# A state-space stage whose side work is moved in its schedule: pieces read two units behind, two silus and the low rank part at other units

## What is computed

```python
xz = x @ Wi.T
xp, z = (xz[..., :d_inner], xz[..., d_inner:])
xp = silu(causal_conv4(xp, conv_w) + conv_b)
dlt, Bp, Cp = split(xp @ Wx.T, [64, 80])         # the low rank part
delta = softplus(dlt @ Wdt.T + bdt)              # the time steps
h[t] = exp(delta[t] * A) * h[t-1] + delta[t] * Bp[t] * xp[t]
y[t] = sum_n Cp[t, n] * h[t, n] + xp[t] * Dp
out = y * silu(z) @ Wo.T
```

## Time and profile before

| | before |
|---|---|
| median of 3 runs | 1148.64 us (1146.84 to 1153.44) |
| profiled execution | 1147.67 us |
| its span | 1145.9 us |
| busy PE / PEld / DVE / ACT / POOL | 873.2 / 561.9 / 883.2 / 631.6 / 735.1 us |
| mean granted clock of TensorE | 0.856 |

### The profile page before, as it was taken

How to read it: one execution, slowest core, us unless ns; L and a number is a source line. 1 busy time by engine, 2 the same in 40 slices (tenths; PEclk the granted TensorE clock), 3 DMA queues, 4 the chain that set the end, 5 groups by cost and what they waited for, 6 DMA issues and landing times. The chain is left out here.

```text
span 1145.9 us, 14984 instructions
## 1 busy us (share of the span) xinstructions
PE 873.2 (76%) x4244; PEld 561.9 (49%) x4244; DVE 883.2 (77%) x1786; ACT 631.6 (55%) x1407; POOL 735.1 (64%) x508
## 2 busy tenths in 40 slices
PE   7897959897989587862899928697979887259920
PEld 4243324333434243432799904365656676259920
DVE  5796999799989999978577755795986977455412
ACT  4878735875587558426344413747385774256610
POOL 0889799889898999920766466665323442047656
PEclk8899989997999898975899958799899977569965
DMA  5644445455445444523233412202001110332223
GB/s 160 186 117 139 150 151 166 128 160 165 138 146 160 151 152 154 170 89 108 61 93 93 80 53 72 64 27 71 21 29 47 47 48 19 105 132 66 68 67 98
DMA packets 90905, 118.95 MB, mean 104 GB/s; under 512 B 12508, under 2 KB 48804, under 8 KB 90696
## 3 DMA queue, kind: packets, MB, share of 16 engines
q1 hardware_dynamic: 84168, 104.34, 29.3%
q0 software_dynamic: 6656, 13.64, 4.9%
HBM read 103.70 MB, written 14.25 MB: 103 GB/s over the span
## 5 line engine op out<-in xcount | busy, mean ns | idle before, releaser
L695 POOL TENSOR_TENSOR ma_bu<-ma_u,ma_row_b 128x1024 f32<-128x1024 f32 x128 | 298.4, 2357 | 9.6 <-DVE ma_u L896 8.0
L415 PE MATMUL y_ps<-ma_h,ident 128*128 128x512 f32 x512 | 259.5, 646 | 26.5 <-POOL ma_h L705 21.5
L570 ACT ACTIVATE decay_ps<-ma_delta,negA 128x512 f32<-128x512 f32 x256 | 172.4, 686 | 83.0 <-DVE ma_h L790 80.1
L1228 POOL DMA_INDIRECT s_rows<-xs,take x112 | 125.3, 1119 | 131.4 <-POOLq L950 83.5
L415 PEld LDWEIGHTS y_ps<-ma_h,ident 128*128 128x128 f32 x512 | 102.3, 208 | 160.1 <-issue 113.4
L1245 PE MATMUL s_up_ps<-s_xt,s_w 128*128 128x128 f32 x896 | 121.3, 280 | 0.0
L780 DVE TENSOR_TENSOR_SCAN decay_ps<-decay_ps,ma_carry,ma_bu 128x512 f32<-128x512 f32 x88 | 110.1, 1271 | 11.2 <-issue 8.4
L1581 POOL TENSOR_TENSOR mi_dec<-mi_dec,mi_gm 128x512 f32<-128x512 f32 x32 | 40.7, 1273 | 120.2 <-DVE mi_gm L2046 107.3
L790 DVE TENSOR_TENSOR ma_h<-decay_ps,ma_row_c 128x512 f32<-128x512 f32 x176 | 117.2, 666 | 0.0
L1245 PEld LDWEIGHTS s_up_ps<-s_xt,s_w 128*128 128x128 f32 x896 | 112.1, 196 | 0.0
L705 POOL TENSOR_TENSOR ma_h<-ma_h,ma_row_c 128x1024 f32<-128x1024 f32 x40 | 97.0, 2425 | 20.6 <-DVE ma_h L780 18.7
(11 more groups left out here) (324 smaller groups left out, 1735.9 us busy)
## 6 DMA issues: line engine op xcount, KB each, us to landing
ma_row_b<-bc_rows SPq DMA_DIRECT2D x128, 256.0 KB, 3.6
ma_row_c<-bc_rows SPq DMA_DIRECT2D x128, 256.0 KB, 3.3
mi_cs<-cs_rows SPq DMA_DIRECT2D x32, 256.0 KB, 3.3
ys<-s_outs SPq DMA_DIRECT2D x28, 256.0 KB
w<-in_experts SPq DMA_DIRECT2D x1, 4112.0 KB, 14.9
w<-in_experts SPq DMA_DIRECT2D x1, 3072.0 KB, 10.9
xs<-rows SPq DMA_DIRECT2D x4, 512.0 KB, 3.4
out<-X SPq DMA_DIRECT2D x8, 256.0 KB, 2.3
```

Of the source, the lines that this page charges most:

```text
L415: mm = pe.matmul(y_ps[:, j, :], m.ident[:], h[g % HS][:, j, :], start=False, stop=True, skip_group_check=True)
L570: act.activation(decay[s % DS][:], delta[b % 2][:, j, col(c)], ACT.Exp, scale=m.negA0[:, j, n:n + 1]).then_inc(decay_done, 1)
L695: pool.tensor_tensor(bu[g % BUS][:], u[b % 2][:, :, col(c)], both(row_b[g % BS]), ALU.mult).then_inc(bu_done, 1)
L1228: pool.indirect_dma_start(rows[s % ROWS][:], None, m.xs[layer], bass.IndirectOffsetOnAxis(ap=m.take[:, s:s + 1], axis=0)).then_inc(fetched ...
```

## The change

Five sets of unit numbers change, and ACT reads the pieces of unit g-2 in its unit g, where it read those of g-1 (across the border of a batch too):

```diff
-    Z, XP = (5, 6, 8, 11), (4, 7, 10, 13)
-    Z_SILU, X_SILU, LOW, V, SOFT, SUM, U = 12, 14, 16, 18, 23, 25, 27
+    Z, XP = (5, 7, 9, 11), (4, 6, 8, 10)
+    X_SILU, Z_SILU, LOW, V, SOFT, SUM, U = 12, 16, 13, 16, 21, 23, 25
+    READ_AFTER = 2
     GATE, OUT, COUNT = (18, 1), (22, 2), (24, 5)
...
-    FIRST_HAT = {2: 9, 3: 17}
-    FIRST_TURN = {2: 14, 3: 24}
+    FIRST_HAT = {2: 9, 3: 23}
+    FIRST_TURN = {2: 20, 3: 27}
...
-                    if s > 0:
-                        for key in pieces(b, s - 1):
+                    if g >= READ_AFTER:
+                        for key in pieces(*divmod(g - READ_AFTER, UNITS)):
                             read_piece(key)
```

## The result

| | before | after |
|---|---|---|
| median of 4 runs each | 1150.35 us (1146.84 to 1153.44) | 1178.1 us (1174.96 to 1182.97) |
| ratio, with 95% interval | | 1.0246 (1.0193 to 1.0299) |
| profiled execution | 1147.67 us | 1174.96 us |
| last gate of the stage starts at | 502.8 us | 524.8 us |
| from there to the end of the span | 643.1 us | 648.4 us |

The change costs 27.75 us by the medians. The sign and the places inside the stage were forecast, the growth behind the stage was not; the size forecast was 18.8 us, and 1178.1 lies above the range's end of 1176.

The account below looks back on a forecast made before the run. DVE was taken to set the pace, so only its idle time and own durations matter. Terms 0.3 + 1.3 + 2.3 + 2.75 + 1.2 + 5.7 + 5.2 = 18.8 us on 1147.7, plus half the median's 1.0, gave 1167; range 1150 to 1176.

Parts of the forecast that it names:

- Silu of x at 12: Batch 1, scan of unit 14: a stall of 4.1 us where it was 2.96, while the 2.82 at unit 16 goes.
- Silu of z at 16, and the v piece ahead of the addition: Batch 1: a stall of 0.9 us at unit 18, then 2.9 at the gate, where it was 0.80.
- the step that gave +0.3: Batch 0 by the same steps as batch 1: stalls of 3.3 + 2.9 + 2.85 = 9.05 us against 8.8.
- Batch 3: Silu of z moves from 12 to 16, onto hat and back pieces: the gate waits 2.75 us, from no stall.
- The clock: PE partly at 1.2 GHz after idling ahead of the gate's addition: 1.3 us at each of four gates, 5.2 in all.
- Batch ends: Ends of batches 1 and 2: additions end 1.35 us behind the gate's due time in both; +1.2 us.
- The sums: Delta sums at units 23 and 24: the first waits for POOL's product, +1.9 us in each of three batches, 5.7.
- The end of this stage carries over one to one: Any shift of the stage's end moves the total equally, as the next stage starts from it.
- waits alone: Rival: only the waits, without lock and clock, as POOL slips out of step and PE stays at 2.4 GHz; about 1156, chance 0.23.
- faster: Rival: silu blocks four units apart are hidden, scan stalls of 16.4 us go, gates cost 8 more; 1140, chance 0.09.
- same: Rival: new stalls at 18 equal those removed at 16, the gate's stall is mostly hidden; 1150 us, chance 0.11.
- six units behind: Rival: PE falls behind for good and DVE waits for free product buffers; 1185 us, chance 0.05.

## Why the prediction was right and where it failed

*What bounds the kernel, and the kinds of stalls*: right. No work was added, DVE waits more, at the places named. One sign of being right did not come: ACT's waits for x pieces mostly stayed (0.68, 2.36 and 3.16 us in batch 1, where it was 1.75, 2.58 and 2.55). Only the last of them stands ahead of a stall of DVE.

*Silu of x at 12*: right. Forecast 4.1 at the scan of unit 14, measured 4.59 and 4.58 (3.56 in batch 0), and the same to 0.01 in the second execution. ACT's read of the last x began at 209.9, forecast 206.6, so 3.3 later. DVE was 3.0 later too (ready for the scan at 211.4, where it was at 208.4), which is why the stall held all the same. PE's first x piece started at 180.78 for 179.44, and its chain took some 2 us more than counted, with waits of 1.19 and 0.60 us for ACT's reads where I had 0.5. The block took 4.6 us, as in the earlier trace rows. Beside it, ScalarE: Activation LUTs (What ACT_TABLE_LOAD costs) of the Trainium skill puts a switch at some 2.66 us with its drain; the rows at 210.62 and 211.91 show 1.28 and a gap of 0.01 us, so no drain stood between them here.

*Silu of z at 16, and the v piece ahead of the addition*: right for batches 1 and 2. Stall at unit 18: 0.9 and 1.1, measured 1.09 twice; gate 2.9 and 2.8 without the clock, measured 3.00 and 3.00 in the kernel with PE kept busy. The claim that the read two units behind would alone end 1 us too late for the gate was right in kind: 1.52 without a silu.

*Batch 0*: the step that gave +0.3 failed (+2.7); 1.8 of the difference is the stall at unit 18, 4.70 for 2.9. The step carried the chain of batch 1 over to batch 0. But there a small piece of the modulation stands in PE's unit 12, and PE idled 3.13 us ahead of it; the next addition took 3.66 us, the low pieces came late (ACT waits 3.23 us for the first at 99.20), the block of z began at 103.25, and the stall at unit 18 was 4.70. Moving that piece took the stall to 0.76, though 2.8 came back at unit 14 and the gate. PE's lag was counted too small here as well: the ring of six was full at unit 17, whose first scan started 0.21 us behind the end of the addition of unit 11 (a wait of 0.19, and of 1.32 in the kernel without a silu of z), where I had found PE four units late at worst. I had seen the piece's wait in the kernel before as a stall of 5.58 and never asked what made it so much larger than the other two.

*Batch 3*: the mechanism was right and the size too small. The gate's wait without the clock is 2.80 (PE kept busy) for 2.75 forecast, but the decay of unit 18 too is late behind the block (1.25), which I had left out: 4.05 in all. PE stood idle 8.37 us ahead of the back piece, since it waited for ACT's read behind the block.

*The clock*: the term was mis-sized and mis-built. I took 1.3 at each of four gates. Against the kernel with PE kept busy, three gates had 1.39, 1.17 and 2.44 and batch 0's had none; in the second execution it was 2.75, 1.14, 0 and 1.58. The sum is 5.0 and 5.5, close to the 5.2, but that is in part luck, since single gates drew 0 to 2.75; and my bound of 1.8 for each was too low, since behind an idle time not only the addition but the small pieces ahead of it and behind it are slow (batch 3: 1.12 for a back piece that took 0.60 at 478.02, 3.62 for the addition, 0.93 for a hat piece that took 0.60 at 460.52). What was missing is that the clock charges other places too: the addition ahead of batch 0's low pieces (3.66 us), one ahead of add_out (3.03 and 3.78 in the two executions, where add_out waits 1.56 and 2.85), and the batch ends in the kernel with PE kept busy. How much of add_out's wait is the clock is not shown.

*Batch ends*: 1.67 each for 1.35. Right, 0.3 short.

*The sums*: the mechanism was right, and only its size was off by where the sum falls. POOL's product started 0.35 us before the sum in batches 1 and 2 (0.4 forecast), and the sum took 3.08 us: +1.88 twice, as forecast. POOL's timeline after:

```profile
254.16 2.35 POOL L706 TENSOR_TENSOR ma_h<-ma_h,ma_row_c 128x1024 f32<-128x1024 f32 x1
```

It ends at 256.5, and the sum at 257.6, 1.1 behind. In batch 0 the wait of 1.56 for add_out came first, and the sum took only 1.42. So 4.0 of 5.7, while that wait itself, which I had not forecast, cost 1.56. By SBUF — State Buffer (Who interferes with whom) of the Trainium skill a VectorE instruction with two SBUF inputs contends with a GpSimd instruction that reads SBUF, through a shared port pair that is an exclusive lock; the trace agrees, with 3.08 beside POOL's product and 1.20 in the kernel with the sums two units later.

*"The end of this stage carries over one to one"*: this step failed. It was a claim on order, and I read it as one on time. The rest took 5.3 us more in the profiled execution, and 2.4 more when both kernels were executed again (645.7 against 643.3). This is the largest single miss. Of the 5.3 us, 2.7 are within what the two executions of the kernel after differ by (the two levels of the second layer), and the range had no room for them: I took the executions of one kernel to differ by the median's offset alone. Whether the other 2.4 to 2.6 come with the change or by chance is open.

*From execution to median*: 3.1 us in the kernel after (1178.1 against 1174.96), where I counted 0.5. The median of 1178.1 stands 11.1 over 1167: 3.2 in the stage, 5.3 in the rest, 2.6 from this. The range reached 9 above the forecast, for the bounds of two costs, and not for what any later part draws.

*Rivals*: "waits alone" fell by the rows at 1.2 GHz and the sums of 3.08; "faster" by the stalls at unit 14; "same" by the gates. PE was six units behind only in batch 0, for 0.19 us, and not for good.

## What to carry to other kernels

Where one engine reads another's results in program order, the distance at which it reads is paid by whatever stands behind the next piece: count the round trip to the last addition ahead of a gate, and let no piece stand between them. Moving a silu block away from one piece puts it on another; so ask at each new place what was awaited there, and for the first batch apart, as its side work differs. And give a loss found in one stage a range that includes the chance variation of the stages behind it, from several executions of the same kernel if there are any.

## What the runs showed of the hardware

The granted clock is not a property of one gap. Behind idle times of PE of 2.8 to 3.1 us the following addition took 1.98 us at a granted clock of 1.00 (batch 0, at 112.87), 3.37 (batch 1, 0.71 over the stretch shown) and 3.66 (batch 0, at 93.79), all in one execution of the kernel after; the gate of batch 0 drew 0 in one execution and 2.75 in the next. With PE kept busy over the gaps the four gates waited 3.00, 3.00, 3.00 and 2.80, and the granted clock was 0.84 in place of 1.00 in a stretch that was not touched. And the second layer, whose code is the same in all these kernels, took 230.1 to 231.6 us in ten executions and 235.4 to 237.4 in seven, while the rest as a whole differed by 4.4 us between two executions of one kernel.
